# Scaling the expert outputs instead of the hidden units, and accumulating them one pass earlier, in a fused Mamba + mixture-of-experts layer

## The chip, the cores and the metric

The program runs on all 8 NeuronCores of one Trainium2 chip, one sequence of 2048 tokens per core, with no exchange between the cores. The metric is the device time of the slowest core in microseconds (us). Engines are named as in the profile: PE is TensorE, DVE is VectorE, ACT is ScalarE, POOL is GpSimd, SP is SyncE, whose queue issues the weight transfers here.

## The reference

One layer: `x = x + LN(mamba(LN(x)))`, then `x = x + LN(ffn(LN(x)))`.

```python
# mamba: 2048 inner channels, 16 states
xz = x @ in_proj_w;  x_, z = split(xz)
x_ = silu(causal_conv4(x_) + conv_b)
B, C, dt = split(x_ @ x_proj_w);  dt = softplus(dt * dt_w + dt_b)
h_t = exp(dt * A) * h_{t-1} + (dt * x_) * B_t          # per channel and state
y = (sum_n h_t[n] * C_t[n] + x_ * D) * silu(z);  return y @ out_proj_w
# ffn: one shared expert and 15 routed ones, 1024 hidden units each, top 3 of 15
shared = relu(x @ sW1 + sb1) @ sW2 + sb2
cw = top-3 of softmax(x @ router_W + router_b), other entries 0      # [token, expert]
h = relu(x @ eW1[e] + eb1[e]);  ye = h @ eW2[e] + eb2[e]
return shared + sum_e ye * cw[:, e]
```

Every expert is computed for every token; `cw` is zero where a token does not use it. A factor that belongs to a token may be applied to `h` or to `h @ eW2[e]`: the product is the same up to rounding.

## The kernel before

Data lies with channels on the partitions and tokens along the free axis. The tokens are worked off in four super-chunks of 512 (index `s`). For each, the mamba part projects two chunks of 256 tokens (`f_mm`, L901), convolves, and then scans: 16 channel groups `g_`, each with 16 states. The feed-forward part of super-chunk `t = s - 1` is woven into the scan of super-chunk `s`, one expert per channel group; the one of the last super-chunk stands alone at the end. So the program has a scan without experts (`s` = 0), three **mixed stages** (`s` = 1, 2, 3), each a loop of 16 passes `k_` = 0 to 15 (L1217), and a **last stage** of experts alone (L1392). There is no scheduler. Each engine works through its own instructions in the order in which the `emit_` functions are called, and waits on counting semaphores (`c_t` of PE, `c_s` of ACT, `c_v` of DVE, one per weight slot for DMA). Because a wait may name an instruction that is written later, the counts are worked out ahead in tables (`relu_layout`, and the block before L1132).

The pieces of one pass:

- `mk_dtda_g` (ACT): two instructions for `dt`, then 16 exponentials `m_da` (L1153) into two buffers. The exponential of state n waits for the scan of state n-2 (L1151).
- `mk_scan_g` (DVE): `m_wdt` (L1169), 16 pairs of `m_dbx` (L1180) and scan (L1184), a copy of the last column (L1188), then what is called the scan's tail below: the products with C, their sum over the states and the gate (L1191 to L1214).
- `emit_w1` (PE): 8 groups of 8 matmuls of 512 columns (L633) into two PSUM banks in turn. Group n waits for the ReLU of group n-2 (L628); the first two of an expert wait for the ReLUs of the expert before.
- `emit_relu` (ACT): 8 ReLUs out of PSUM into `f_he` (L655), then a copy of the token factors of this expert, spread over the partitions, from PSUM into `f_cwrep` (L661).
- `emit_scale` (DVE): one multiplication of all of `f_he` (128x4096) by `f_cwrep` (L670). The shared expert, `e` = 0, has none.
- `emit_w2` (PE): 8 groups of 8 matmuls (L702) into two other PSUM banks. Group n waits for the accumulation of group n-2 (L699). For experts 0 and 15 each group has a ninth matmul for the biases (L709, L713).
- `emit_acc` (DVE): 8 additions of a bank to `f_acc` (L735); for expert 0 a copy (L732).
- `emit_cwrep` (PE): one matmul (L608) that spreads the token factors over the partitions, into `p_st`.
- `emit_fwa`, `emit_fwb` (SP): the weights. An expert has four halves A, B (first matrix) and C, D (second matrix), 1 MB each, in four DMAs of 256 KB. They go round three slots, so a half may be loaded when the half three places back has been used: D of an expert, and A of the next, when its first-matrix matmuls are done; B and C of the next when its second-matrix matmuls are done. `emit_w2` waits for C and D before its first matmul.

The order of calls in a pass of a mixed stage (L1217 to L1231):

```python
mk_dtda_g(k_);  emit_relu(_t, k_ - 1);  mk_scan_g(k_)
emit_acc(_t, k_ - 2);  emit_scale(_t, k_ - 1)           # from k_ = 2 on
emit_w2(_t, k_ - 1);  emit_fwa(_t, k_);  emit_cwrep(_t, k_)
emit_w1(_t, k_);  emit_fwb(_t, k_)
```

On DVE this reads: scan of group k, accumulation of expert k-2, scaling of expert k-1. On PE: second matrix of expert k-1, first matrix of expert k.

Of the kernel before, what the change touches and what calls it, by code (L numbers as in the profile page):

```python
# [45 lines left out]
def build_program():  # L46
# [48 lines left out]
    with st:  # L95
# [146 lines left out]
        with ms:  # L242
# [36 lines left out]
            f_cwrep = msb("f_cwrep", (128, TF), BF16)  # L279
# [132 lines left out]
            def emit_ffn_pre(t, s):  # L412
# [32 lines left out]
                def f3_norm(v, t=t):  # L445
# [96 lines left out]
            def relu_layout(t, snap, interleaved):  # L542
# [4 lines left out]
                for e in range(16):  # L547
                    start = snap + dt18 * min(e + 2, 16) + sum(relub(m) for m in range(e))
# [96 lines left out]
            def emit_relu(t, e):  # L645
                def f(s_, t=t, e=e):
# [11 lines left out]
                    if e >= 1:  # L658
                        s_.wait_ge(c_t.h, tk[("cwrepps", t, e)])
                        assert tk[("cwrepe", t, e)] == c_s.inc(  # L660
                            s_.copy(f_cwrep[:], p_st[:, 0:TF]))  # L661
                        tk[("cwrepe2", t, e)] = tk[("cwrepe", t, e)]
# [3 lines left out]
            def emit_scale(t, e):  # L666
                def f(v, t=t, e=e):
                    v.wait_ge(c_s.h, tk[("reludone", t, e)])
                    bcast = f_cwrep[:].unsqueeze(1).broadcast_to((128, NH, TF))
                    tok = c_v.inc(v.tensor_mul(f_he[:], f_he[:], bcast))  # L670
                    if ("scale", t, e) in tk:
                        assert tk[("scale", t, e)] == tok
                    else:
                        tk[("scale", t, e)] = tok
                block.vector(f)

            def emit_w2(t, e, s):
                def f(t_, t=t, e=e, s=s):
# [4 lines left out]
                    if e >= 1:  # L683
                        t_.wait_ge(c_v.h, tk[("scale", t, e)])
                    else:
                        t_.wait_ge(c_s.h, tk[("reludone", t, e)])
# [36 lines left out]
            def emit_acc(t, e):  # L723
                def f(v, t=t, e=e):
                    if e == 0 and t >= 1:
                        v.wait_ge(c_v.h, tk[("fout", t - 1, ND - 1)])
                    for dmg in range(4):
                        for j in range(2):
# [5 lines left out]
                            else:  # L734
                                tok = c_v.inc(v.tensor_add(  # L735
                                    f_acc[:, m, :], p_proj[:, 1024 + j * TF:1024 + (j + 1) * TF],
                                    f_acc[:, m, :]))
                            if ("accvh", t, e, dmg, j) in tk:
                                assert tk[("accvh", t, e, dmg, j)] == tok
                            else:  # L740
                                tk[("accvh", t, e, dmg, j)] = tok
                block.vector(f)

            def emit_ffn_post(t, s):
                def f4_sq(s_, t=t):
                    s_.wait_ge(c_v.h, tk[("accvh", t, 15, 3, 1)])
# [25 lines left out]
                def f4_fin(v, t=t):  # L772
# [31 lines left out]
            for c in range(NCH):  # L804
# [296 lines left out]

                _pos = c_v.n
                for k_ in range(NG):
                    tk[("wdt", sc_i, k_)] = _pos + 1
# [6 lines left out]
                    if _t is not None and k_ >= 2:  # L1111
                        for dmg in range(4):
                            for jj in range(2):
                                tk[("accvh", _t, k_ - 2, dmg, jj)] = _pos + 2 * dmg + jj + 1
                        _pos += 8
                        tk[("scale", _t, k_ - 1)] = _pos + 1
                        _pos += 1
                if _t is not None:
                    for dmg in range(4):
                        for jj in range(2):  # L1120
                            tk[("accvh", _t, NG - 2, dmg, jj)] = _pos + 2 * dmg + jj + 1
                    _pos += 8
                    tk[("scale", _t, NG - 1)] = _pos + 1
                    _pos += 1
                    for dmg in range(4):
                        for jj in range(2):
                            tk[("accvh", _t, NG - 1, dmg, jj)] = _pos + 2 * dmg + jj + 1
                    _pos += 8
# [346 lines left out]
```

## Time and profile before

| | us |
|---|---|
| median of 2 runs (8704.58 and 8708.09) | 8706.33 |
| profiled execution, its own time | 8700.44 |
| its span, slowest core (core 5) | 8698.9 |
| span of the fastest core (core 2) | 8662.2 |
| DVE busy | 3524.8 (41%) |
| PE busy | 3133.4 (36%) |
| ACT busy | 2016.7 (23%) |
| DVE, PE, DMA and ACT in the chain that ended last | 34%, 29%, 18%, 9% |

No engine is busy for half of the span, so the busy table names no bound. The chain that ended last changes hands between DVE, PE, DMA and ACT, and must be read within a pass. In the timelines a row such as "x48" merges instructions of one line that follow each other; its second number is their time together. The bracket at its end gives the idle time of that engine before it and what ended it. Records of PE overlap by some tenths of a us.

### The profile page before, as it was taken

To read this page: it belongs to the slowest core of one execution; us is meant where nothing else is said; L and a number is where in the kernel's file an instruction comes from. 1 tells how busy PE (TensorE), PEld (TensorE's weight loads), DVE (VectorE), ACT (ScalarE), POOL (GpSimd) and SP (SyncE) were. 2 spreads that over 40 slices of the span, in tenths; PEclk is the share of its full clock that TensorE was granted. 3 is DMA by queue.
4 is the path that set the end of the run, shared out by engine and by line. 5 is a ranking of instruction groups with operands and counts; after the bars stand their busy time and mean duration, and the time that the engine had idled before them with its cause. 6 is when DMAs were issued, how large, how long until landed. Compare 5 with 4: busy or idle time off the path is not lost.

```text
span 8698.9 us, 47147 instructions; the slowest of 8 cores (8662.2 to 8698.9 us)
## 1 busy us (share of the span) xinstructions
PE 3133.4 (36%) x11876; PEld 1261.7 (15%) x11876; DVE 3524.8 (41%) x5093; ACT 2016.7 (23%) x2925; POOL 187.4 (2%) x380
## 2 busy tenths in 40 slices
PE   0000310013323434453324434353324344364776
PEld 0000100001101111111101111121101111121332
DVE  0000168852165465522165564522265555622112
ACT  2000233321232222211232222211232222212111
POOL 0320000000000000000000000000000000000000
PEclk9999999985556767675556667675557676677887
DMA  4899200001101111111101111121101111121222
GB/s 155 115 119 119 63 2 4 3 17 46 46 20 49 58 39 58 49 56 44 50 10 58 49 49 58 39 64 44 52 10 58 46 51 49 49 78 49 87 97 73
DMA packets 281131, 473.92 MB, mean 54 GB/s; under 512 B 35695, under 2 KB 138353, under 8 KB 275713
## 3 DMA queue, kind: packets, MB, share of 16 engines
q1 hardware_dynamic: 255394, 366.03, 13.2%
q0 software_dynamic: 25472, 104.88, 8.2%
q8 instruction: 103, 1.69, 0.1%
q14 instruction: 162, 1.33, 0.1%
HBM read 521.10 MB, written 88.08 MB: 70 GB/s over the span
## 4 chain that ended last, share of the span: by engine, by line
DVE 34%; PE 29%; DMA 18%; ACT 9%; issue 7%; SPq 2%; DVEq 1%; POOL 0%; ACTq 0%; POOLq 0%
DVE h_buf L1184 15%; PE p_proj L633 11%; DMA w_kt<-scr_in 11%; PE p_proj L702 10%; DVE m_dbx L1180 5%; DMA f_wb<-scr_e 4%; PE p_proj L901 4%; DVE h_buf L1191 3%; DVE conv_acc L961 2%; DMA w_kt<-scr_out 1%; DVE h_buf L1200 1%; DVE h_buf L1195 1%; PE p_proj L1292 1%; SPq L577 1%; DVE h_buf L1197 1%
## 5 line engine op out<-in xcount | busy, mean ns | idle before, releaser
L702 PE MATMUL p_proj<-f_he,f_wb 128*128 128x512 bf16 x4096 | 1132.5, 444 | 1922.3 <-DVE f_acc L735 1412.5
L633 PE MATMUL p_proj<-f_xln,f_wb 128*128 128x512 bf16 x4096 | 1046.3, 421 | 590.9 <-DMA f_wb<-scr_e 360.4
L1153 ACT ACTIVATE m_da<-m_dtg,k_a 128x512 f16<-128x512 f16 x1024 | 731.8, 721 | 1289.9 <-DVE h_buf L1184 1280.2
L1184 DVE TENSOR_TENSOR_SCAN h_buf<-m_da,h_last,m_dbx 128x512 f16<-128x512 f16 x768 | 985.5, 1283 | 82.5 <-DVE m_dbx L1180 3.2
L901 PE MATMUL p_proj<-m_xln,w_kt 128*128 128x256 bf16 x2048 | 491.7, 409 | 993.0 <-DMA w_kt<-scr_in 790.6
L702 PEld LDWEIGHTS p_proj<-f_he,f_wb 128*128 128x128 bf16 x4096 | 440.3, 110 | 2598.1 <-issue 2278.1
L670 DVE TENSOR_TENSOR f_he<-f_he,f_cwrep 128x4096 bf16<-128x4096 bf16 x60 | 137.5, 2292 | 1401.0 <-ACT f_cwrep L661 1401.0
L956 DVE TENSOR_SCALAR conv_acc<-u_pre,k_conv_w 128x256 f16<-128x256 bf16 x128 | 35.8, 280 | 1417.6 <-ACT u_pre L928 742.6
L633 PEld LDWEIGHTS p_proj<-f_xln,f_wb 128*128 128x128 bf16 x4096 | 427.6, 106 | 1197.7 <-issue 823.2
L735 DVE TENSOR_TENSOR f_acc<-p_proj,f_acc 128x512 bf16<-128x512 f32 x480 | 328.1, 690 | 657.5 <-PE p_proj L702 590.5
L655 ACT ACT_TABLE_LOAD x64 | 82.1, 1283 | 2172.8 <-PE p_proj L633 2172.7
L1180 DVE TENSOR_TENSOR m_dbx<-m_wdt,brep 128x512 f16<-128x512 f16 x1024 | 435.5, 425 | 129.0 <-ACT m_da L1153 23.9
L1292 PE MATMUL p_proj<-z_s,w_kt 128*128 128x512 bf16 x512 | 164.5, 461 | 732.4 <-DVE z_s L1214 644.2
L655 ACT ACTIVATE f_he<-p_proj,k_eb 128x512 bf16<-128x512 f32 x480 | 327.2, 687 | 412.5 <-PE p_proj L633 411.7
L901 PEld LDWEIGHTS p_proj<-m_xln,w_kt 128*128 128x128 bf16 x2048 | 234.8, 130 | 1249.9 <-issue 1175.7
L1184 DVE TENSOR_TENSOR_SCAN h_buf<-m_da,m_dbx 128x512 f16<-128x512 f16 x256 | 313.7, 1225 | 27.5 <-DVE m_dbx L1180 1.4
L1191 DVE TENSOR_TENSOR h_buf<-h_buf,crep 128x2048 f16<-128x2048 f16 x256 | 296.5, 1221 | 6.7
L325 DVE TENSOR_SCALAR rowa<-p_st 1x256 f32<-1x256 f32 x16 | 6.6, 412 | 578.8 <-PE p_st L318 578.8
L928 ACT ACT_TABLE_LOAD x32 | 41.1, 1283 | 731.9 <-PE p_proj L901 731.9
L961 DVE SCALAR_TENSOR_TENSOR conv_acc<-u_pre,k_conv_w,conv_acc 128x253 f16<-128x253 bf16 (+2 forms) x384 | 185.4, 483 | 41.4 <-DVE conv_acc L967 0.9
L930 ACT ACT_TABLE_LOAD x32 | 41.1, 1283 | 626.8 <-PE p_proj L901 626.8
L1292 PEld LDWEIGHTS p_proj<-z_s,w_kt 128*128 128x128 bf16 x512 | 48.3, 109 | 851.7 <-issue 831.8
(146 smaller groups left out, 2251.3 us busy)
## 6 DMA issues: line engine op xcount, KB each, us to landing
f_wb<-scr_e SPq DMA_DIRECT2D x1024, 256.0 KB, 4.4
w_kt<-scr_in SPq DMA_DIRECT2D x512, 128.0 KB, 2.0
scr_e<-e_w POOLq DMA_DIRECT2D x240, 256.0 KB, 141.1
cast_stage<-w_in POOLq DMA_DIRECT2D x8, 2048.0 KB, 10.7
w_kt<-scr_out SPq DMA_DIRECT2D x128, 128.0 KB, 2.0
scr_in<-cast_bf SPq DMA_DIRECT2D x64, 128.0 KB
cast_stage<-w_out POOLq DMA_DIRECT2D x16, 512.0 KB, 4.5
out<-f_out POOLq DMA_DIRECT2D x32, 256.0 KB, 2.6
```

The lines of the kernel that those rows point to most:

```text
L633: inst = t_.matmul(p_proj[:, j * TF:(j + 1) * TF], f_wb[:, hs, k % 4, (hmg * 2 + j) * 128:(hmg * 2 + j + 1) * 128], f_xln2[:, k, :], start ...
L655: s_.activation(f_he[:, m, :], p_proj[:, j * TF:(j + 1) * TF], ACT.Relu, bias=b1[:, m:m + 1]))
L670: tok = c_v.inc(v.tensor_mul(f_he[:], f_he[:], bcast))
L702: inst = t_.matmul(p_proj[:, 1024 + j * TF:1024 + (j + 1) * TF], f_wb[:, hsC if k < 4 else hsD, k % 4, (dmg * 2 + j) * 128:(dmg * 2 + j + ...
L735: tok = c_v.inc(v.tensor_add(f_acc[:, m, :], p_proj[:, 1024 + j * TF:1024 + (j + 1) * TF], f_acc[:, m, :]))
L901: inst = t.matmul(p_proj[:, j * 512:j * 512 + TC], w_kt[:, wpar, j * 128:(j + 1) * 128], m_xln[:, k, :], start=(k == 0), stop=(k == 7))
L961: t1 = c_v.inc(v.scalar_tensor_tensor(conv_acc[:, cp, off:TC], xp(g_, 0, TC - off), k_conv_w[:, g_, kk:kk + 1], conv_acc[:, cp, off:TC], A ...
L1153: s.activation(m_da[:, dpar, :], m_dtg[:], ACT.Exp, scale=k_a[:, g_, n:n + 1]))
L1180: v.tensor_mul(m_dbx[:], m_wdt[:], brep[:, n, :]))
L1184: v.tensor_tensor_scan(h_buf[:, n, :], m_da[:, dpar, :], m_dbx[:], init, AL.mult, AL.add))
L1191: t1 = c_v.inc(v.tensor_mul(h_buf[:, 4 * q:4 * q + 4, :], h_buf[:, 4 * q:4 * q + 4, :], crep[:, 4 * q:4 * q + 4, :]))
L1292: inst = t.matmul(p_proj[:, j * SC:(j + 1) * SC], w_kt[:, wpar, j * 128:(j + 1) * 128], y_g[:, k, :], start=(k == 0), stop=(k == NG - 1))
```

## The change

The factor is applied to the output of an expert instead of to its hidden units. `emit_scale` is gone. In `emit_acc`, for e >= 1, each of the 8 additions becomes two instructions: `y_tmp = bank * f_cwrep` and, after a wait for it, `f_acc = y_tmp + f_acc`. PE's wait for a free bank is on the first of the two. `emit_w2` waits for the ReLUs and the copy of `f_cwrep` (`reludone`), no longer for the scaling. `f_cwrep` has two buffers, and the copy into it waits from expert 3 on for the accumulation of expert e-2. A new token `accdone` stands where the last addition was waited for. `emit_acc`, `f3_norm` and `f4_fin` begin with a wait of DVE for its own last instruction, since they write `y_tmp`.

Together with this the order of the calls changes, in the mixed stages and in the last stage.

```diff
@@ emit_relu @@
+                        if e >= 3:
+                            s_.wait_ge(c_v.h, tk[("accdone", t, e - 2)])
                         assert tk[("cwrepe", t, e)] == c_s.inc(
-                            s_.copy(f_cwrep[:], p_st[:, 0:TF]))
+                            s_.copy(f_cwrep[:, e % 2, :], p_st[:, 0:TF]))
@@ emit_scale @@
-                    v.wait_ge(c_s.h, tk[("reludone", t, e)])
-                    bcast = f_cwrep[:].unsqueeze(1).broadcast_to((128, NH, TF))
-                    tok = c_v.inc(v.tensor_mul(f_he[:], f_he[:], bcast))
@@ emit_w2 @@
-                    if e >= 1:
-                        t_.wait_ge(c_v.h, tk[("scale", t, e)])
-                    else:
-                        t_.wait_ge(c_s.h, tk[("reludone", t, e)])
+                    t_.wait_ge(c_s.h, tk[("reludone", t, e)])
+                    if e == 0:
@@ emit_acc @@
+                    v.wait_ge(c_v.h, _vn)
...
                             else:
-                                tok = c_v.inc(v.tensor_add(
-                                    f_acc[:, m, :], p_proj[:, 1024 + j * TF:1024 + (j + 1) * TF],
-                                    f_acc[:, m, :]))
+                                bc = f_cwrep[:, e % 2, :]
+                                tok = c_v.inc(v.tensor_mul(
+                                    y_tmp[:], p_proj[:, 1024 + j * TF:1024 + (j + 1) * TF], bc))
+                                v.wait_ge(c_v.h, tok)
+                                c_v.inc(v.tensor_add(f_acc[:, m, :], y_tmp[:], f_acc[:, m, :]))
+                                v.wait_ge(c_v.h, c_v.n)
+                    tk[("accdone", t, e)] = c_v.n
@@ the loop of a mixed stage @@
                 for k_ in range(NG):
-                    mk_dtda_g(k_)
                     if _t is not None and k_ >= 1:
                         emit_relu(_t, k_ - 1)
-                    mk_scan_g(k_)
-                    if _t is not None and k_ >= 2:
-                        emit_acc(_t, k_ - 2)
-                        emit_scale(_t, k_ - 1)
+                    mk_dtda_g(k_)
                     if _t is not None:
+                        emit_cwrep(_t, k_)
                         if k_ >= 1:
                             emit_w2(_t, k_ - 1, sc_i)
                         emit_fwa(_t, k_)
-                        emit_cwrep(_t, k_)
                         emit_w1(_t, k_, sc_i)
                         emit_fwb(_t, k_)
+                    if _t is not None and k_ >= 1:
+                        emit_acc(_t, k_ - 1)
+                    mk_scan_g(k_)
```

The loop of the last stage is changed in the same way (ReLUs of k-1, `emit_cwrep`, second matrix of k-1, weights and first matrix of k, accumulation of k-1).

What this does to the order on the engines follows. DVE, between the scan of one channel group and the next, in the middle of a mixed stage; before:

```order
L1214 TENSOR_TENSOR z_s<-y_tmp,z_s 128x512
L742 UNCONDITIONAL_BRANCH
L735 TENSOR_TENSOR f_acc<-p_proj,f_acc 128x512 x8
L675 UNCONDITIONAL_BRANCH
L670 TENSOR_TENSOR f_he<-f_he,f_cwrep 128x4096
L1215 UNCONDITIONAL_BRANCH
L1169 TENSOR_TENSOR m_wdt<-m_dtg,x_post 128x512
```

and after the change (the pair of L733 and L737 stands there 8 times, of which two are shown):

```order
L1212 TENSOR_TENSOR z_s<-y_tmp,z_s 128x512
L740 UNCONDITIONAL_BRANCH
L733 TENSOR_TENSOR y_tmp<-p_proj,f_cwrep 128x512
L737 TENSOR_TENSOR f_acc<-y_tmp,f_acc 128x512
L733 TENSOR_TENSOR y_tmp<-p_proj,f_cwrep 128x512
L737 TENSOR_TENSOR f_acc<-y_tmp,f_acc 128x512
```

The eight additions have become eight pairs, and the multiplication of `f_he` is gone. By the calls in the loop, what stood here was the accumulation of expert k-2 and the scaling of expert k-1, after the scan of group k; now it is the accumulation of expert k, between the scans of groups k and k+1.

ACT at the start of a mixed stage, before. `m_spt`, `m_dtg` and `m_da` belong to a channel group, `f_he` (with `k_sb`, the shared expert's bias) to expert 0:

```order
L1138 ACTIVATE m_spt<-m_dtr,k_dtb,k_dtw 128x512
L1143 ACTIVATE m_dtg<-m_spt 128x512
L1153 ACTIVATE m_da<-m_dtg,k_a 128x512 x16
L1157 UNCONDITIONAL_BRANCH
L1138 ACTIVATE m_spt<-m_dtr,k_dtb,k_dtw 128x512
L1143 ACTIVATE m_dtg<-m_spt 128x512
L1153 ACTIVATE m_da<-m_dtg,k_a 128x512 x16
L664 UNCONDITIONAL_BRANCH
L655 ACTIVATE f_he<-p_proj,k_sb 128x512 x8
L1157 UNCONDITIONAL_BRANCH
```

and after:

```order
L1136 ACTIVATE m_spt<-m_dtr,k_dtb,k_dtw 128x512
L1141 ACTIVATE m_dtg<-m_spt 128x512
L1151 ACTIVATE m_da<-m_dtg,k_a 128x512 x16
L669 UNCONDITIONAL_BRANCH
L658 ACTIVATE f_he<-p_proj,k_sb 128x512 x8
L1155 UNCONDITIONAL_BRANCH
L1136 ACTIVATE m_spt<-m_dtr,k_dtb,k_dtw 128x512
L1141 ACTIVATE m_dtg<-m_spt 128x512
L1151 ACTIVATE m_da<-m_dtg,k_a 128x512 x16
```

Before, the exponentials of groups 0 and 1 both stand ahead of the ReLUs of expert 0; now only those of group 0 do, and the ReLUs of expert k stand between the exponentials of groups k and k+1.

PE in the middle of a mixed stage, before (L702 second matrix, L608 token factors, L633 first matrix):

```order
L721 UNCONDITIONAL_BRANCH
L702 MATMUL p_proj<-f_he,f_wb 128x512 x64
L611 UNCONDITIONAL_BRANCH
L608 MATMUL p_st<-f_cwTb,k_sel 128x512
L643 UNCONDITIONAL_BRANCH
L633 MATMUL p_proj<-f_xln,f_wb 128x512 x64
```

and after (L695 second matrix, L611 token factors, L636 first matrix):

```order
L614 UNCONDITIONAL_BRANCH
L611 MATMUL p_st<-f_cwTb,k_sel 128x512
L714 UNCONDITIONAL_BRANCH
L695 MATMUL p_proj<-f_he,f_wb 128x512 x64
L646 UNCONDITIONAL_BRANCH
L636 MATMUL p_proj<-f_xln,f_wb 128x512 x64
```

The one matmul for the token factors has moved from between the two matrices to ahead of the second. The rows of the SP queue, which issues the weights, stand in the same order as before.

## Rows read from the trace of the kernel before

**Rows 1.** Windows: us, PE, PEld, DVE, ACT, POOL busy, granted clock, DMA share, GB/s.

```profile
2443.30:3773.00 1329.70, 557.77 (x2069) 219.43 (x2067) 734.68 (x862) 338.69 (x460) 0.00 (x0) 0.70 0.15 49
7925.00:8652.00 727.00, 525.65 (x2079) 214.20 (x2077) 122.94 (x143) 120.86 (x169) 0.00 (x0) 0.85 0.27 88
3442.60:3453.10 10.50, 10.50 (x48) 4.60 (x48) 0.00 (x0) 3.87 (x6) 0.00 (x0) 1.00 0.00 0
3459.60:3462.90 3.30, 3.28 (x8) 1.15 (x9) 2.88 (x5) 1.44 (x2) 0.00 (x0) 0.50 0.34 130
```

**Rows 2.** Who waited for whom: us in total, times, longest.

```profile
ACT L655 <- PE p_proj L633: 2172.7, 61, 40.6
PE p_proj L702 <- DVE f_acc L735: 1412.5, 39, 37.5
DVE f_he L670 <- ACT f_cwrep L661: 1401.0, 60, 24.6
```

**Rows 3.** Timeline, one pass of the first mixed stage: start, us, engine, line.

```profile
3405.53 0.17 DVE L1188 COPY h_last<-h_buf 128x16 f16<-128x16 f16 x1
...
3417.69 13.07 PE L702 MATMUL p_proj<-f_he,f_wb 128*128 128x512 bf16 x48 [37.02 <-DVE f_acc L735]
...
3437.01 5.05 PE L633 MATMUL p_proj<-f_xln,f_wb 128*128 128x512 bf16 x16 [5.93 <-DMA f_wb<-scr_e]
...
3442.60 10.52 PE L633 MATMUL p_proj<-f_xln,f_wb 128*128 128x512 bf16 x48 [0.54 <-ACT f_he L655]
...
3454.84 2.29 DVE L670 TENSOR_TENSOR f_he<-f_he,f_cwrep 128x4096 bf16<-128x4096 bf16 x1 [23.27 <-ACT f_cwrep L661]
...
3457.33 0.43 DVE L1169 TENSOR_TENSOR m_wdt<-m_dtg,x_post 128x512 f16<-128x512 f16 x1 [0.20 <-ACT m_dtg L1143]
...
3459.62 5.69 PE L702 MATMUL p_proj<-f_he,f_wb 128*128 128x512 bf16 x16 [6.50 <-DMA f_wb<-scr_e]
...
3488.94 0.18 DVE L1188 COPY h_last<-h_buf 128x16 f16<-128x16 f16 x1
```

**Rows 4.** Timeline, start of the first mixed stage, DVE, ACT and PE.

```profile
2443.27 0.42 DVE L1169 TENSOR_TENSOR m_wdt<-m_dtg,x_post 128x512 f16<-128x512 f16 x1 [5.10 <-ACT m_dtg L1143]
...
2486.64 0.42 DVE L1169 TENSOR_TENSOR m_wdt<-m_dtg,x_post 128x512 f16<-128x512 f16 x1
...
2514.73 1.28 ACT L655 ACT_TABLE_LOAD   x1
...
2516.86 12.93 PE L633 MATMUL p_proj<-f_xln,f_wb 128*128 128x512 bf16 x48 [72.27 <-ACT f_he L655]
...
2517.83 0.18 DVE L1188 COPY h_last<-h_buf 128x16 f16<-128x16 f16 x1
...
2536.55 3.57 PE L702 MATMUL p_proj<-f_he,f_wb 128*128 128x512 bf16 x8 [6.76 <-DMA f_wb<-scr_e]
```

**Rows 5.** Timeline, end of the first mixed stage, start and end of the third.

```profile
3773.29 0.69 DVE L735 TENSOR_TENSOR f_acc<-p_proj,f_acc 128x512 bf16<-128x512 f32 x1 [1.46 <-PE p_proj L713]
...
6385.66 0.43 DVE L1169 TENSOR_TENSOR m_wdt<-m_dtg,x_post 128x512 f16<-128x512 f16 x1 [5.10 <-ACT m_dtg L1143]
...
7700.12 3.39 PE L702 MATMUL p_proj<-f_he,f_wb 128*128 128x512 bf16 x8 [6.47 <-DMA f_wb<-scr_e]
...
7718.99 0.69 DVE L735 TENSOR_TENSOR f_acc<-p_proj,f_acc 128x512 bf16<-128x512 f32 x1 [1.46 <-PE p_proj L713]
```

**Rows 6.** PE group, 7990 to 8620 us (last stage): busy, mean ns, idle before.

```profile
L702 PE MATMUL p_proj<-f_he,f_wb 128*128 128x512 bf16 x896 | 224.4, 417 | 89.4 <-DMA f_wb<-scr_e 89.4
```

**Rows 7.** Timeline, VectorE in the last stage.

```profile
7990.90 2.29 DVE L670 TENSOR_TENSOR f_he<-f_he,f_cwrep 128x4096 bf16<-128x4096 bf16 x1 [23.21 <-ACT f_cwrep L661]
```

**Rows 8.** Groups by line on DVE, whole execution.

```profile
L735 DVE TENSOR_TENSOR f_acc<-p_proj,f_acc 128x512 bf16<-128x512 f32 x480 | 328.1, 690 | 657.5 <-PE p_proj L702 590.5 <-PE p_proj L713 67.0
...
L1214 DVE TENSOR_TENSOR z_s<-y_tmp,z_s 128x512 bf16<-128x512 f16 x64 | 27.2, 425 | 6.7
...
L782 DVE TENSOR_TENSOR y_tmp<-f_acc,p_rep 128x512 f16<-128x512 bf16 x32 | 22.0, 688 | 37.3 <-DMA out<-f_out 20.0 <-PE p_rep L408 16.6
```


## Prediction before the run

> **What bounds the kernel now.** I read the busy time by stage first. In a mixed stage of 1329.7 us no engine is busy for more than 735 us; the last stage has 525.7 us of PE in 727 [rows 1]. So the mixed stages are bound by waits, and the question is who waits for whom. The largest waits are three sides of one circle [rows 2]: ACT's ReLUs wait 2172.7 us for the first-matrix matmuls, PE's second-matrix matmuls wait 1412.5 us for the accumulation on DVE (39 times, up to 37.5 us, which is nearly a whole scan), and DVE's scaling waits 1401.0 us for the token factors, which ACT writes behind the last ReLU. DVE waits while PE works, and PE waits while DVE scans.
>
> The timeline of one pass shows it as a chain without overlap [rows 3]. From the end of the scans (3405.53, L1188) to the next one (3488.94) are 83.4 us:
>
> - tail of the scan on DVE, then the first two additions, until PE may go on: 3405.53 to 3417.69, 12.2
> - six of the eight groups of the second matrix: 13.1
> - wait for weight half B (5.93 idle): 3430.7 to 3437.0, 6.3
> - all of the first matrix: 3437.0 to 3453.1, 16.1
> - last ReLU, copy of the factors: until 3454.84, 1.7
> - scaling 2.3 and the gap to the next `m_wdt`: until 3457.33, 2.5
> - 16 scans: until 3488.94, 31.6
>
> Only two groups of the second matrix (3459.62, x16) lie beside the scans. Three mixed stages hold 1330.7 us (2443.27 [rows 4] to 3773.98 [rows 5]) and 1334.0 (6385.66 to 7719.68 [rows 5]); the middle one I take as the first. Together 3995.4.
>
> **The change, part by part.** The decisive edit is the distance. Before, the ReLUs of expert k stand behind the exponentials of group k+1 and its accumulation behind the scan of group k+2. Now the ReLUs stand behind the exponentials of group k and the accumulation ahead of the scan of group k+1. One expert is finished for one scan, as before, but another part of it lies beside the scan. The new pass can be read from the old trace, because expert 0 already runs this way up to its second matrix [rows 4]:
>
> - `m_wdt` at 2486.64 to the end of the 16th exponential, where ACT takes the ReLU table at 2514.73: 28.1. ACT is ahead with `dt` and two exponentials there, as it will be always, since it finishes the ReLUs a whole second matrix before DVE is free. The scans end at 2517.83, 3.1 later; 28.1 + 3.1 is 0.4 less than the 31.6 above, where DVE ran ahead of ACT at first.
> - table load and first ReLU, which frees a bank: PE goes on at 2516.86, 2.1
> - six groups of the first matrix, 48 matmuls: 12.9
> - wait for half D: PE starts at 2536.55, so 6.8 from the end of the first matrix; in the last stage the same wait is 89.4 us in 14, 6.4 each [rows 6]. I take 6.5.
> - all of the second matrix, 64 matmuls: 224.4 us in 14, 16.0 each [rows 6]
> - last bank: multiplication, addition, two gaps of 0.1, then `m_wdt`: 1.3
>
> Sum 28.1 + 2.1 + 12.9 + 6.5 + 16.0 + 1.3 = 66.9 us for a pass that took 83.4. What goes: the tail of the scan with the last 3 us of scans, 14.4 us, now beside the first matrix; the scaling, 2.3; the last ReLU and copy, 1.7, now under the wait for D. What comes: 2.1 for the release and 1.3 for the last pair. The exposed weight wait changes from B to D; B now lands, with two groups of the first matrix behind it (6.3 + 5.8 us), inside the 28 us of scans.
>
> What is late next: DVE's tail takes 11.4 us (the 12.2 above without one addition of 0.7 and a gap), so it ends at about 2517.83 + 11.4 = 2529.2 in rows 4, and the first bank of the second matrix is full only at 2536.55 + 3.6 = 2540.1. The tail has 11 us to spare; without that cover up to 11 us of a pass would come back.
>
> Edits with small prices. The multiplication of a PSUM bank by `f_cwrep` is not in the trace. L782 has its operand types (a 16-bit tile and a PSUM bank into f16), 688 ns; L735, also out of PSUM, takes 690; the lower end is 425 (L1214, no PSUM). I take 690. The addition of an f16 and a bf16 tile is like L1214, f16 with bf16: 425; the upper end is 690 [rows 8]. A pair takes 0.69 + 0.1 + 0.42 + 0.1 = 1.3 us, at most 1.6, and PE fills a bank in 8 x 0.219 = 1.75 at its fastest (48 matmuls in 10.50 [rows 1]). So seven pairs of eight hide behind PE and only the last is on the path; at the upper end it costs 0.3 more in each of 48 passes, 13 us. The matmul for the token factors ahead of the second matrix waits for the copy, 1.3 us behind the last ReLU's start, and lies under the wait for D: nothing. The waits of DVE for itself: 0.1 us at most each, 20 in a stage, 2 us; the new wait of ACT for `accdone` of two experts before is long over. SP issues the same transfers in the same order.
>
> The stage: first scan 28.1; expert 0 (66.9 with 18.9 instead of 16.0 for its 72 matmuls, as from 7700.12 to 7718.99 [rows 5], and 0.8 instead of 1.3 for the copy) 69.3; 14 passes of 66.9, 936.6; the last expert, without a scan, 2.1 + 12.9 + 6.5 + 18.9 + 1.2 = 41.6. Sum 1075.6, three times 3226.8, which is 768.6 less than 3995.4.
>
> The last stage: scaling is removed there 15 times, and I count nothing. It ends at 7990.90 + 2.29 = 7993.2 [rows 7], and yet all the 89.4 us that PE is idle ahead of the second matrix end with a DMA [rows 6]: half D, which may start only when the first matrix is done. The 2.3 us lie under that wait. Only the last pair adds 0.5.
>
> 8700.4 (own time of the profiled execution) - 768.6 + 0.5 = 7932.3. The median of the runs lies 5.9 above that execution: **7938 us**, 8.8% faster.
>
> **Bounds.** Wait for D: 6.0 to 7.4 in single rows like those of B (5.93 in rows 3, 6.76 in rows 4), so about +-0.8 x 48 = 40 us. The 64 matmuls: 48 take 12.9 to 13.1 from the lower clock and 10.5 at the full one [rows 1, 3, 4], so 64 lie between 14.0 and 17; -35 to +45 us over the stages. Last pair +13. In the steady passes nothing else is unseen. The likeliest case spans 7860 to 8035.
>
> **Rivals.**
>
> *More of the matmuls at the lower clock, or a longer wait for weights.* The granted clock is 0.50 (1.2 GHz) in the first 3.3 us of a burst after idle time and 1.00 (2.4 GHz) later in it [rows 1]; a matmul costs 0.21 us more at the lower level. Now 112 matmuls of a pass are exposed instead of 112 in other places, with one idle gap of the same kind ahead of each matrix, so I expect the same share. Against a change speaks the last stage, denser than a mixed one will be, with a mean clock of 0.85 and the same waits at 88 GB/s. If 22 more of them ran slowly, or the weights came 4.6 us later, a pass would take 71.5: 8160 us.
> The Trainium skill, "TensorE: Matmul & The Clock Gate", section "Seeing it yourself", says that three or more cores of a die with dense matmuls are held to 13/16 of the full clock, which would speak against packing the work of 8 cores closer. By that rule the 91 matmuls at full rate in a pass would take 0.23 x 0.219 us more each, an estimate of 4.6 us per pass and 8160 in all. The trace of before does not agree: with all 8 cores in the last stage the bursts stand at 1.00.
>
> *No overlap in fact.* If the first matrix could go on only after DVE's tail, by a wait that I have overlooked, a pass would be 12.3 us longer (14.4 less 2.1), over 48 passes 590: 8528 us. Against it: PE restarts at 2516.86 while the tail runs until 2529 [rows 4].
>
> *Slower: the clock stays down.* In a burst PE is at the full level only after some time of work. If the new pattern (16 matmuls, a gap, 48, a gap of 6.5, 64) never lifts it, the 91 fast matmuls of a pass cost 0.21 more each, 19.1 us, and 48 passes 917: 8855, slower by 1.7%. If the whole program is held down, the last stage's 16 experts add 22 us each, 352: 9207, slower by 5.8%. It decides against the change from 75 further slow matmuls in a pass on. Against it: 48 matmuls after a long gap already take 13.1 rather than 20.5 [rows 3].
>
> *The change doesn't do what it says.* If the pair on DVE were slower than PE's 1.75 us for a bank, PE would wait at each bank. It would need 0.45 us more than the nearest rows give; even at 2.2 us a pair the eight cost 3.6 a pass, 173 in all: 8111.
>
> **How the numbers follow.** The forecast has 84%. More slow matmuls, later weights or slow pairs (8110 to 8160 and up to 8300): 10%. No overlap: 4%, about half of it on either side of the bound. Slower clock: 2%, half of it above 2%. Faster or slower by 2% is about what a measurement of this kernel can tell. That gives 0.96 faster, 0.03 within 2%, 0.01 slower. The range 7860 to 8090 takes in the bounds of the likeliest case and the nearer part of the second.
>
> **What would show it.** A pass of 67 us between two L1188-type copies in a mixed stage, 1076 us per stage. PE's wait for DVE falls from 1412 us to next to nothing in the mixed stages; in its place PE waits for the ReLUs, once per pass, for some 15 us of scans. DVE waits for the second matrix 24 us a pass. Waits for f_wb stay near 6.4 ahead of the second matrix, and those ahead of the first lie beside scans. The last stage stays at 727. I am wrong if the pass is over 70 us, if PE's 48 and 64 take more than 13.5 and 17, if the first group of the second matrix waits for DVE's tail, or if the last stage moves by more than 10 us.

## The result, and the profile after

The changed kernel takes 7996.35 us (median of 11 runs, 7934.0 to 8086.81), the kernel before 8732.18 (10 runs, 8701.92 to 8781.87). The ratio is 0.9143, 95% interval 0.9109 to 0.9177: 8.6% faster. The forecast was 7938, so the likeliest case came about, 58 us above its value and inside its range. The profiled execution took 7979.56 us where the sum had 7932.3. The ratio leaves out, on both sides, the executions in which one die was clearly slower.

The spans of the cores of the profiled execution:

```profile
core 0: 7910.4 us, clock 0.664
...
core 7: 7978.0 us, clock 0.656
die 0 (median of its cores): 7929.8 us, clock 0.683
die 1 (median of its cores): 7962.3 us, clock 0.678
```

The cores of die 0 end at 7910 to 7940, where the sum put them; those of die 1 at 7951 to 7978. So there are two readings to make: why the pass is as forecast, and what die 1 adds. First the pass, in the timeline of core 7 in the first mixed stage, beside [rows 3]; columns as there:

```profile
3346.01 0.18 DVE L1186 COPY h_last<-h_buf 128x16 f16<-128x16 f16 x1
...
3357.00 0.42 DVE L1212 TENSOR_TENSOR z_s<-y_tmp,z_s 128x512 bf16<-128x512 f16 x1
...
3363.98 15.38 PE L695 MATMUL p_proj<-f_he,f_wb 128*128 128x512 bf16 x64 [4.21 <-DMA f_wb<-scr_e]
...
3367.37 0.69 DVE L733 TENSOR_TENSOR y_tmp<-p_proj,f_cwrep 128x512 f16<-128x512 f32 x1 [9.95 <-PE p_proj L695]
3368.17 0.43 DVE L737 TENSOR_TENSOR f_acc<-y_tmp,f_acc 128x512 bf16<-128x512 f16 x1
3369.10 0.69 DVE L733 TENSOR_TENSOR y_tmp<-p_proj,f_cwrep 128x512 f16<-128x512 f32 x1 [0.51 <-PE p_proj L695]
...
3380.26 0.43 DVE L737 TENSOR_TENSOR f_acc<-y_tmp,f_acc 128x512 bf16<-128x512 f16 x1
3380.86 0.43 DVE L1167 TENSOR_TENSOR m_wdt<-m_dtg,x_post 128x512 f16<-128x512 f16 x1 [0.17 <-DVE f_acc L737]
...
3386.03 5.93 PE L636 MATMUL p_proj<-f_xln,f_wb 128*128 128x512 bf16 x16 [6.67 <-ACT m_da L1151]
...
3408.95 1.28 ACT L658 ACT_TABLE_LOAD   x1
...
3411.08 12.26 PE L636 MATMUL p_proj<-f_xln,f_wb 128*128 128x512 bf16 x48 [19.12 <-ACT f_he L658]
3412.05 0.18 DVE L1186 COPY h_last<-h_buf 128x16 f16<-128x16 f16 x1
...
3424.85 0.37 PE L611 MATMUL p_st<-f_cwTb,k_sel 15*128 15x512 bf16 x1 [1.51 <-ACT f_cwrep L666]
...
3430.03 2.29 PE L695 MATMUL p_proj<-f_he,f_wb 128*128 128x512 bf16 x5 [4.81 <-DMA f_wb<-scr_e]
```

What the reader is to see: from `h_last` to `h_last` are now 66.04 us. From `m_wdt` (3380.86) to the ReLU table (3408.95) are 28.1; PE goes on 2.1 later, at 3411.08, while the scan's tail still runs. The tail ends 11.4 after `h_last` (3357.42) and the first bank is full 9.95 later, so the cover holds. Seven of the eight pairs end 0.51 us before the next bank is full; only the eighth is on the path. Half B, 6.67 us of waiting ahead of 3386.03, lies inside the scans. (The row names an exponential as the releaser, which the first matrix does not need; in the first experiment below the same row reads 6.32 <-DMA f_wb.) The wait for D, 6.7 us from 3423.34 to 3430.03, now shows in two parts, since the matmul for the token factors stands in it: 1.51 for ACT's copy and 4.81 for the transfer.

The waits of the slowest core, beside [rows 2]: who waited for whom, us in total, times, longest.

```profile
DVE y_tmp L733 <- PE p_proj L695: 1139.4, 448, 34.1
PE p_proj L636 <- ACT f_he L658: 983.6, 55, 29.7
...
PE p_proj L695 <- DMA f_wb<-scr_e: 251.9, 54, 6.6
```

The second matrix no longer waits for DVE; its 1412.5 us in [rows 2] have no successor. The circle is cut: apart from the weight transfers, PE waits at one place of a pass, for the ReLU behind the scan, and DVE at one, for the second matrix. The new pair by its groups, beside [rows 8] (busy, mean ns of one, idle before):

```profile
L733 DVE TENSOR_TENSOR y_tmp<-p_proj,f_cwrep 128x512 f16<-128x512 f32 x480 | 332.1, 692 | 1231.7 <-PE p_proj L695 1139.4
...
L737 DVE TENSOR_TENSOR f_acc<-y_tmp,f_acc 128x512 bf16<-128x512 f16 x480 | 204.2, 425 | 50.9 <-DVE y_tmp L733 1.4
```

What die 1 adds on cores 6 and 7 stands in windows over the last stage, from the first to the last write of `f_acc`: core 0, then core 7 and one burst of core 7 (columns as in [rows 1]).

```profile
7165.24:7858.83 693.59, 502.94 (x1965) 206.95 (x2003) 139.66 (x248) 108.41 (x150) 0.00 (x0) 0.85 0.27 90
```

```profile
7185.34:7926.59 741.25, 557.41 (x2005) 217.55 (x2003) 139.61 (x248) 108.64 (x150) 0.00 (x0) 0.76 0.25 84
7586.60:7599.50 12.90, 12.90 (x50) 5.18 (x48) 0.00 (x0) 4.12 (x6) 0.00 (x0) 0.81 0.00 1
```

The same stage takes 47.7 us longer on core 7, at a mean granted clock of 0.76 instead of 0.85, with the same bytes moved (90 GB/s in 693.6 us, 84 in 741.3) and equal DVE and ACT time. In the burst the clock stands at 0.81 and a matmul takes 12.90 / 50 = 0.258 us, where a burst at 1.00 takes 10.50 / 48 = 0.219 [rows 1]. Summed over the clock record of each core, this third level lasts 292 to 450 us on cores 4 to 7, and does not occur on cores 0 to 3, nor on any core in the trace of before. On cores 4 and 5 it stands elsewhere, above all in the first mixed stage, whose passes take 69.5 and 69.2 us there, while their last stage is as short as core 0's (693.9 and 690.9). There a second matrix of core 4 takes 19.0 us, with a window at 0.81 inside it:

```profile
2613.51 19.01 PE L695 MATMUL p_proj<-f_he,f_wb 128*128 128x512 bf16 x64 [4.53 <-DMA f_wb<-scr_e]
```

```profile
2619.00:2632.50 13.50, 13.50 (x52) 5.39 (x50) 6.70 (x12) 0.00 (x0) 0.00 (x0) 0.81 0.01 2
```

### The profile page after: what moved, and what is told of

The parts are those of the page before. It is cut to its first block, busy times and chain, and to the rows that moved or that the text cites. A ratio compares the mean times of both kernels' runs of the same rounds, so it can differ in the third digit from the quotient of the medians.

```text
span 7978.0 us, 48591 instructions; the slowest of 8 cores (7910.4 to 7978.0 us)
## 1 busy us (share of the span) xinstructions
PE 3191.3 (40%) x11876; PEld 1274.8 (16%) x11876; DVE 3599.0 (45%) x5513; ACT 2014.3 (25%) x2925; POOL 187.4 (2%) x380
## 4 chain that ended last, share of the span: by engine, by line
PE 33%; DVE 30%; DMA 19%; ACT 9%; issue 7%; SPq 2%; DVEq 1%; POOL 0%; ACTq 0%; POOLq 0%
DVE h_buf L1182 15%; PE p_proj L695 13%; DMA w_kt<-scr_in 12%; PE p_proj L636 11%; DVE m_dbx L1178 5%; PE p_proj L902 4%; DMA f_wb<-scr_e 4%; DVE conv_acc L962 2%; DMA w_kt<-scr_out 1%; DVE h_buf L1189 1%; PE p_proj L1287 1%; ACT L658 1%; DMA cast_stage<-w_out 1%; DMA scr_in<-cast_bf 1%; SPq L593 1%
## 5 line engine op out<-in xcount | busy, mean ns | idle before, releaser
L636 PE MATMUL p_proj<-f_xln,f_wb 128*128 128x512 bf16 x4096 | 1165.4, 455 | 1356.2 <-ACT f_he L658 983.6
L695 PE MATMUL p_proj<-f_he,f_wb 128*128 128x512 bf16 x4096 | 1070.0, 428 | 292.4 <-DMA f_wb<-scr_e 251.9
L733 DVE TENSOR_TENSOR y_tmp<-p_proj,f_cwrep 128x512 f16<-128x512 f32 x480 | 332.1, 692 | 1231.7 <-PE p_proj L695 1139.4
L636 PEld LDWEIGHTS p_proj<-f_xln,f_wb 128*128 128x128 bf16 x4096 | 453.2, 113 | 2066.6 <-issue 1816.8
L695 PEld LDWEIGHTS p_proj<-f_he,f_wb 128*128 128x128 bf16 x4096 | 429.5, 107 | 904.5 <-issue 600.1
L737 DVE TENSOR_TENSOR f_acc<-y_tmp,f_acc 128x512 bf16<-128x512 f16 x480 | 204.2, 425 | 50.9 <-DVE y_tmp L733 1.4
L1287 PEld LDWEIGHTS p_proj<-z_s,w_kt 128*128 128x128 bf16 x512 | 47.7, 108 | 849.8 <-issue 829.6
```

What stands on the lines that cost most here:

```text
L636: inst = t_.matmul(p_proj[:, j * TF:(j + 1) * TF], f_wb[:, hs, k % 4, (hmg * 2 + j) * 128:(hmg * 2 + j + 1) * 128], f_xln2[:, k, :], start ...
L695: inst = t_.matmul(p_proj[:, 1024 + j * TF:1024 + (j + 1) * TF], f_wb[:, hsC if k < 4 else hsD, k % 4, (dmg * 2 + j) * 128:(dmg * 2 + j + ...
L733: tok = c_v.inc(v.tensor_mul(y_tmp[:], p_proj[:, 1024 + j * TF:1024 + (j + 1) * TF], bc))
L737: c_v.inc(v.tensor_add(f_acc[:, m, :], y_tmp[:], f_acc[:, m, :]))
L1287: inst = t.matmul(p_proj[:, j * SC:(j + 1) * SC], w_kt[:, wpar, j * 128:(j + 1) * 128], y_g[:, k, :], start=(k == 0), stop=(k == NG - 1))
```

## The experiments

A "pass" below is the mean distance of two `h_last` copies, from the third to the last of a mixed stage; in the kernel before it is 83.8 to 84.1 us (core 5), in the changed one 66.7 to 67.1 (core 0). "The last stage" is taken from the first to the last write of `f_acc`: 695.8 on core 5 before, 693.6 on core 0 of the changed kernel, and between 689 and 703 in both kernels on every core that has no 0.81 there.

**The order alone.** The new order of calls, with `emit_scale` of expert k-1 kept, placed ahead of the accumulation, and the old single addition. Against the changed kernel:

```diff
+                        if k_ >= 2:
+                            emit_scale(_t, k_ - 1)
                         emit_acc(_t, k_ - 1)
@@ emit_w2 @@
-                    t_.wait_ge(c_s.h, tk[("reludone", t, e)])
+                    if e >= 1:
+                        t_.wait_ge(c_v.h, tk[("scale", t, e)])
```

> The new order, but the factor is applied to the hidden units as before (one multiplication of 128x4096 on VectorE, 2.29 us, ahead of the accumulation of the same expert; one addition per bank). Theory A (the order does everything, the moved multiplication nothing): the 2.3 us lie under the wait for weight half D, which lasts 6.5 us from the end of the first matrix, while ReLU, copy and scaling need 1.3 + 2.3 = 3.7; the last bank costs 0.8 instead of 1.3. So it is 20 to 30 us faster than the changed kernel or equal to it: 7910 to 7960, ratio to before 0.910 to 0.915. Rival B (taking the scaling away was worth its 2.3 us a pass): 110 us slower than the changed kernel, about 8050 to 8090, ratio 0.925.

Measured: 7910.56 us (4 runs), ratio 0.906 (0.9024 to 0.9095); pass 65.8 to 66.4 us. The order brings the whole gain. Its timeline shows why the scaling is free there (core 3):

```profile
3286.33 0.58 ACT L666 CAST f_cwrep<-p_st 128x512 bf16<-128x512 f32 x1
...
3287.01 2.29 DVE L676 TENSOR_TENSOR f_he<-f_he,f_cwrep 128x4096 bf16<-128x4096 bf16 x1 [2.30 <-ACT f_cwrep L666]
...
3292.36 15.31 PE L705 MATMUL p_proj<-f_he,f_wb 128*128 128x512 bf16 x64 [4.83 <-DMA f_wb<-scr_e]
...
3307.78 0.69 DVE L742 TENSOR_TENSOR f_acc<-p_proj,f_acc 128x512 bf16<-128x512 f32 x1 [1.03 <-PE p_proj L705]
3308.39 0.41 DVE L1175 TENSOR_TENSOR m_wdt<-m_dtg,x_post 128x512 f16<-128x512 f16 x1
```

The scaling ends at 3289.30; PE starts at 3292.36, released by the transfer of half D: 3.1 us to spare. And after the last bank one addition stands where the changed kernel has a pair, 0.5 us less in each pass. This kernel's interval lies below that of the changed one, though part of the distance is the clock: 0.81 does not occur in this trace. Its cores span 7874 to 7909 us, the cores of the changed kernel that are without 0.81 7910 to 7940: some 30 us, of which the last pair explains 48 x 0.5 = 24. That is Theory A.

**The scaling alone.** The old order, with the factor applied in `emit_acc` and `emit_scale` gone:

```diff
                         emit_acc(_t, k_ - 2)
-                        emit_scale(_t, k_ - 1)
```

> The old order, but the factor applied to the outputs: pair of multiplication and addition per bank, no multiplication of the hidden units. Theory A: between the copy of the factors (ends 3454.4 in the pass read before) and the next m_wdt (3457.3) ACT needs a table load, 0.81 and 0.63 us for dt anyway, so DVE then waits for dt instead of scaling; in the last stage the scaling lies under the wait for D. Equal to before within 0.3%, ratio 0.997 to 1.003. Rival B: 2.3 us less in 45 passes, ratio 0.988, and 0.984 if the last stage gains as well.

Measured: 8810.61 us (10 runs), ratio 1.0058 (1.0022 to 1.0095), a little above the 0.997 to 1.003 that I had expected, and far from the rival's 0.988. The distance is of the size of the clock's: its trace has 0.81 on all eight cores, and on core 1 a pass takes 83.8 us in the first mixed stage, without that level, and 85.1 in the other two, with it. Its two shortest executions, 8711.3 and 8715.9 us, lie within 0.2% of the 8700.4 of the trace of before. Core 1:

```profile
3455.29 0.58 ACT L666 CAST f_cwrep<-p_st 128x512 bf16<-128x512 f32 x1
3455.88 1.28 ACT L1132 ACT_TABLE_LOAD   x1
...
3458.08 0.63 ACT L1137 ACTIVATE m_dtg<-m_spt 128x512 f16<-128x512 f16 x1
3458.81 0.43 DVE L1163 TENSOR_TENSOR m_wdt<-m_dtg,x_post 128x512 f16<-128x512 f16 x1 [25.41 <-ACT m_dtg L1137]
```

DVE has no scaling to do, and still starts the scan 3.5 us after the start of the copy: it now waits for ACT, which made `m_dtg` under the scaling before (there `m_wdt` waited 0.20 for it, [rows 3]). The 2.3 us are replaced by a wait, and in the old order, too, removing the scaling gained nothing.

**A fourth weight slot**, on the changed kernel: `hs` is taken modulo 4, so the wait for D goes. Room for it comes from the small row tiles, which share memory with `h_buf`.

```diff
-            f_wb = msb("f_wb", (128, 3, 4, 1024), BF16)
+            f_wb = msb("f_wb", (128, 4, 4, 1024), BF16)
-                    hs = (4 * e + 3) % 3
+                    hs = (4 * e + 3) % 4
```

> The changed kernel with four weight slots instead of three (small row tiles share memory with h_buf to make room), so that half D no longer waits for the first matrix of its own expert and B not for the second matrix of the one before. If the wait for D is what stands on the path: a pass falls from 66 us by 4.6 (only ReLU, copy and the one matmul stay between the matrices, 1.9 instead of 6.5) and by 2.1 because the second matrix then starts at the higher clock: 59 to 61 us, 48 passes 290 us. The last stage falls from 45 to 30 or 31 us an expert, 230 us. Sum 7400 to 7480, ratio 0.850 to 0.860. If a third level of the granted clock (0.81, seen in the trace of the changed kernel on cores 4 to 7) takes hold under the denser work: up to 100 us more. Rival (weights bound by the transfer itself, 4 MB an expert at the rate seen, not by the slots): last stage stays above 40 us an expert, ratio above 0.88.

Measured: 7445.88 us (5 runs), ratio 0.8515 (0.8491 to 0.8539); pass 61.5, last stage 478. This beats both kernels, and its ratio is the expected one, though the pass is 0.5 us above the 59 to 61 forecast. The wait was 5.5 to 7.3 us of a pass (core 0 of the changed kernel), and 5.4 come off. What remains of the gap is ACT's copy of the factors and the clock. Two passes of core 1, on the die whose trace has no 0.81, and windows over their second matrices:

```profile
3114.10 0.37 PE L614 MATMUL p_st<-f_cwTb,k_sel 15*128 15x512 bf16 x1 [1.51 <-ACT f_cwrep L669]
3114.62 15.66 PE L698 MATMUL p_proj<-f_he,f_wb 128*128 128x512 bf16 x64 [0.15 <-issue]
...
3176.13 0.37 PE L614 MATMUL p_st<-f_cwTb,k_sel 15*128 15x512 bf16 x1 [1.51 <-ACT f_cwrep L669]
3176.57 13.97 PE L698 MATMUL p_proj<-f_he,f_wb 128*128 128x512 bf16 x64
```

```profile
3114.60:3117.80 3.20, 3.18 (x9) 1.24 (x10) 0.00 (x0) 2.95 (x5) 0.00 (x0) 0.57 1.01 324
3117.80:3130.20 12.40, 12.40 (x57) 5.56 (x56) 7.82 (x14) 0.38 (x1) 0.00 (x0) 0.97 0.18 67
```

```profile
3176.60:3190.50 13.90, 13.90 (x65) 6.34 (x66) 7.82 (x14) 3.36 (x5) 0.00 (x0) 1.00 0.42 137
```

I had expected the second matrix to keep the full clock. It does in the second of these passes; in the first its first 3.2 us run at 0.57 after the same 1.51 us of idle PE. On this core 13.97 and 15.66 alternate from pass to pass in all three mixed stages; why they do stays open.

**A third instruction for each bank.** The multiplication is issued twice, into the same tile, so the result is the same:

```diff
                                     y_tmp[:], p_proj[:, 1024 + j * TF:1024 + (j + 1) * TF], bc))
+                                v.wait_ge(c_v.h, tok)
+                                tok = c_v.inc(v.tensor_mul(
+                                    y_tmp[:], p_proj[:, 1024 + j * TF:1024 + (j + 1) * TF], bc))
```

> The changed kernel with the multiplication of each bank done twice; the bank is released by the second. It doubles the suspected cost on VectorE: a bank takes 2.1 us there instead of 1.3, more than the 1.73 in which TensorE fills one. Theory A (seven of eight pairs hide behind TensorE, up to its pace): in a mixed pass 8 x 2.1 + 3.6 = 20.4 us from the start of the second matrix to the end of the accumulation instead of 17.3, in the last stage 1.4 us an expert; +150 to 180 us over the changed kernel, ratio to before about 0.935. Rival B (accumulation not hidden, each instruction counts): 0.79 x 8 x 60 = 380 us, ratio 0.958. Rival C (all hidden but the last): +40 us, ratio 0.919.

Measured: 8184.74 us (4 runs), ratio 0.9359 (0.9313 to 0.9404); pass 70.6, last stage some 30 us longer. That is 188 us over the changed kernel, a little more than Theory A's 150 to 180 and far from the 380 and 40 of the rivals. One bank on core 5:

```profile
3140.72 0.69 DVE L736 TENSOR_TENSOR y_tmp<-p_proj,f_cwrep 128x512 f16<-128x512 f32 x1
3141.52 0.43 DVE L740 TENSOR_TENSOR f_acc<-y_tmp,f_acc 128x512 bf16<-128x512 f16 x1
3141.56 1.89 PE L695 MATMUL p_proj<-f_he,f_wb 128*128 128x512 bf16 x8 [0.30 <-DVE y_tmp L736]
3142.12 0.69 DVE L733 TENSOR_TENSOR y_tmp<-p_proj,f_cwrep 128x512 f16<-128x512 f32 x1 [0.17 <-DVE f_acc L740]
...
3143.75 1.89 PE L695 MATMUL p_proj<-f_he,f_wb 128*128 128x512 bf16 x8 [0.30 <-DVE y_tmp L736]
```

Now DVE sets the pace and PE waits at each bank: 2.19 us from PE's start on one to the next (3141.56, then 3143.75) instead of 1.73. 8 x 0.46 = 3.7 us, which is the pass's growth. So a pair has about half a us to spare on each bank, and the rival of slow pairs is a real one, a single instruction away.

**The fourth slot in the old order** (the same edit on the kernel before):

> The kernel before with four weight slots (row tiles share memory with h_buf, as in e3), nothing else. Old order, scaling of the hidden units. In a mixed pass the wait for B (6.3) and the slow start of the first matrix (2.1) go, the wait for D lies beside the scans anyway: 83.4 - 8.4 = 75 us, 45 passes 380. In the last stage an expert takes 13.9 + 13.9 for the matrices, 1.7 for ReLU and copy, 2.3 for the scaling: 32 instead of 45, 210. Sum 8110, ratio 0.93. If the order's gain stands by itself, e3 stays 600 us and more below this kernel. Rival (the two edits gain from the same idle time): the gap between them shrinks to below 400.

Measured: 8213.32 us (4 runs), ratio 0.9385 (0.9334 to 0.9437); pass 75.5, last stage 531 to 534 on the cores without 0.81 there. The second matrix still waits for DVE, as long as before [rows 2]:

```profile
PE p_proj L705 <- DVE f_acc L738: 1518.2, 39, 39.4
```

So a weight slot does not replace the change: by the ratios, order and output scaling together are worth 0.9385 - 0.8515 = 0.087 of the time before with four slots, and 0.086 with three. The last stage is some 55 us longer than that of the fourth slot on the changed kernel (478), more than the 1 to 2 us an expert that I had counted; the next experiment tells which of the two edits that is.

**The fourth slot with the scaling kept** (the first experiment's kernel with the same edit):

> e1 with four weight slots: new order, factor applied to the hidden units, no wait for D to hide it. Now the scaling should be on the path: second matrix starts 1.35 + 2.3 = 3.7 us after the first instead of 1.9, and the last bank saves 0.5, so a mixed pass is 1.3 us longer than in e3, 58 us in all, and an expert of the last stage 1.8, 27 us: 7446 + 85 = about 7530, ratio 0.861, where without the fourth slot the same edit made the kernel faster by 30 to 50 us. Rival (scaling hidden here too, or too small to see): equal to e3 or faster.

Measured: 7683.55 us (4 runs), ratio 0.8798 (0.8742 to 0.8853); pass 64.9, last stage 532. The direction is as expected, the size two to three times as large: 3.4 us a pass over the output scaling, not 1.3, and some 180 to 190 us in all on cores without 0.81 (spans of 7610 to 7639 us, where the fourth slot on the changed kernel has 7428 to 7451), not 85. Core 1:

```profile
3135.65 2.29 DVE L679 TENSOR_TENSOR f_he<-f_he,f_cwrep 128x4096 bf16<-128x4096 bf16 x1 [2.28 <-ACT f_cwrep L669]
3135.80 0.37 PE L614 MATMUL p_st<-f_cwTb,k_sel 15*128 15x512 bf16 x1 [1.51 <-ACT f_cwrep L669]
...
3138.27 16.66 PE L708 MATMUL p_proj<-f_he,f_wb 128*128 128x512 bf16 x64 [2.10 <-DVE f_he L679]
```

```profile
3138.30:3144.50 6.20, 6.20 (x17) 2.23 (x18) 0.69 (x1) 1.43 (x3) 0.00 (x0) 0.56 0.56 202
3144.50:3154.90 10.40, 10.40 (x50) 4.71 (x49) 4.15 (x6) 0.00 (x0) 0.00 (x0) 1.00 0.01 2
```

The wait for the scaling is 2.1 us, and the matrix behind it takes 16.66 instead of 15.66 or 13.97, because 6.2 us of it run at 0.56 rather than 3.2 or none. I had priced the wait and not the matmuls that it slows. Over the pass: 1.9 us more between the matrices (3.9 instead of 2.0), 1.8 more for the second matrix (16.65 instead of the mean of 13.97 and 15.66), 0.5 less at the last bank, 3.2 of the 3.4.

With this the four kernels can be compared edit by edit. The order alone, with the scaling of the hidden units kept, is worth 1 - 0.906 = 0.094 of the time before with three slots, and 0.9385 - 0.8798 = 0.059 with four: order and slot gain in part from the same idle time. The output scaling is worth nothing with three slots (it costs the 0.5 us a pass) and 0.8798 - 0.8515 = 0.028 with four. And the last stage takes 531 to 534 us in the old order and 532 in the new one when the scaling is kept: its 55 us belong to the scaling, not to the order.

**The changed kernel once more**, on another chip, for the clock:

> The changed kernel again, for a second trace of it and for runs beside the two above. If the granted clock of 0.81 on cores 4 to 7 belongs to the change, it stands in this trace too, in the same stage; if it comes and goes with the execution (e1 had none, e2 had it on all cores, e6 on cores 0 to 3), the trace shows it elsewhere or not at all, and cores without it span 7900 to 7940 us.

Measured: 8007.7 us (4 runs), ratio 0.913 (0.9061 to 0.9198). Its cores:

```profile
core 1: 8006.7 us, clock 0.693
...
core 5: 7931.0 us, clock 0.763
...
die 0 (median of its cores): 7993.5 us, clock 0.693
die 1 (median of its cores): 7925.2 us, clock 0.662
```

Here die 0 is the longer one, with 544 to 610 us at 0.81 on each of its cores, and die 1 has none. The pass on core 5 is 66.7 to 67.1. So the third level is not tied to a die or to a place in the program. In both traces two neighbouring cores have it in the same stretch of the program, and the other two of the die in another, of nearly the same length. By the clock records, the changed kernel's first trace has it from 1862 to 3134 us of core 4's span and from 6652 to 7923 of core 6's, 1272 and 1271 us from its first to its last; this one from 2475 to 3670 on core 2 and from 6447 to 7676 on core 0, 1195 and 1229 us. Each trace counts from its own core's start, so no run shows whether the four cores had it at one time.

## Why the prediction was right, and where it was not

- **The pass, 83.4 to 66.9.** The passes measured 66.7 to 67.1 in the mean of a stage (core 0). Term by term, forecast and the pass above on core 7, which is a short one of 66.0: scans 28.1, 28.1; table and ReLU 2.1, 2.1; 48 matmuls 12.9, 12.3; wait for D 6.5, 6.7; 64 matmuls 16.0, 15.4 (15.2 to 16.9 on core 0, 16.1 in the mean of its first mixed stage); last pair 1.3, 1.5. Reading the new pass from the start of the stage, where expert 0 already ran that way [rows 4], gave the scans, the release, the 48 matmuls and the wait for D; the last stage gave the 64 matmuls [rows 6].
- **The stage, 1075.6.** From the first `m_wdt` to the last `f_acc` core 0 has 1075.6, 1078.0 and 1071.4, together 3225 against 3226.8; core 7 3232.
- **What goes: "the scaling, 2.3".** The total was right and the attribution wrong. I had put the scaling's 2.3 us a pass, 45 x 2.3 = some 104 us, among what goes, and for the last stage I had written that it lies under the wait for D; the same holds for every mixed pass in the new order. The order alone is no slower than the whole change (0.906 against 0.9143), and the scaling alone gains nothing (1.0058). The gain is the order's; the output scaling costs 0.5 us a pass at the last pair.
- **Pairs behind PE.** 0.69 + 0.43 and two gaps, as worked out; the third instruction shows where that cover ends.
- **"DVE waits for the second matrix 24 us a pass".** In the pass above it waits 9.95 + 7 x 0.5 = 13.5. The 24 is about the time from the tail to the last bank, from which the seven pairs in between are not taken off. It is not in the sum. PE's wait for the ReLUs is 19.1 in the pass above, not "some 15".
- **Two sums that don't close.** What goes and what comes in a pass add up to 15.0 us net (18.4 less 3.4), where 83.4 - 66.9 is 16.5: the two additions ahead of the second matrix and some gaps are not listed. The forecast doesn't use that list. And 64 matmuls in 14.0 instead of 16.0 us would be 96 us less in 48 passes, not 35, so the likeliest case by its own terms reached down to about 7800; the measured time lies at its other side.
- **"The last stage stays at 727", within 10.** On the cores without 0.81 there it does (693.6 on core 0 against 691.3 on core 0 before, by the `f_acc` writes). On core 7 it is 45 us longer than the 695.8 of before's slowest core. This is the rival that I had put inside 10%, more matmuls below full rate, come about in part on one die. Its price by the trace is 3232 - 3227 = 5 us in the mixed stages and 45 in the last, 50 us, where the profiled execution lies 47 above the sum. The rule of the Trainium skill that I weighed ("TensorE: Matmul & The Clock Gate", section "Seeing it yourself") gives 13/16 of the full clock, 0.8125, when three or more cores of a die run dense matmuls; the level in these traces is that one. It was wrong of me to let the trace of before speak against it outright: one execution without the level did not show that the next has none, and the trace doesn't show either that the cores of a die were in their dense stages at one time. It is also not always there: in the same execution cores 0 to 5 run this last stage without it.
- Whether the change makes the third level more frequent stays open. It occurs in the traces of five kernels, old order and new, and not in those of before, of the order alone and of the fourth slot with the scaling kept; one trace each decides nothing. The median's 58 us above the forecast is of the size that it costs, and the spans that are listed for each execution bear this out: in the two in which both dies need the same time the slowest core takes 7934.0 and 7940.9 us, and 7937.2 in the one such execution of the repetition, where the forecast was 7938; in the others one die is 30 us or more behind the other. Only spans and mean clocks are listed, so that the third level is at work in each of those is inferred. The rival "no overlap in fact" was not built; the row at 3411.08, with the tail running until 3423, excludes it.

## What to carry to other kernels

In a program of in-order engines ask which pass's work each call issues, and draw one pass of the new order from a place in the old trace where it already runs (a stage's first pass, its last stage); that gave this forecast within 1%. Before an operation is credited with its own duration, look at what releases the instruction behind it: 2.3 us on DVE were worth nothing here in either order, and 3.4 us a pass, in the new order, once the transfer above them was gone. And take waits away in the order in which they cover each other; order and output scaling, with a fourth slot, reach 7445.9 us, 0.8515 of the time before.

## What the runs showed of the hardware

- A third level of TensorE's granted clock, 0.81, on all cores of one die in one execution of the changed kernel, on those of the other die in another execution on another chip, and on all eight in the traces of the scaling alone and of the fourth slot in the old order; 0.26 us for a 128x512 matmul where 1.00 gives 0.22. The same core of the same kernel spans 7978.0 us with it and 7927.9 without (core 7), 7976.6 and 7910.4 (core 0): 50 to 66 us, up to nearly a per cent, so small differences are to be read from the passes of cores without it.
- A gap costs more than its length. After 1.5 us of idle PE, a small matmul and no further wait, the second matrix took 13.97 or 15.66 us; with 2.1 us of wait more, 16.66 (16.5 to 16.7 in nearly all mixed passes of that core, 15.66 in the first of each stage and in most of the last stage). The difference goes with the time for which the mean granted clock stood near 0.56: none, 3.2 and 6.2 us.
